# Spreading the side work of the attention stage over its pairs, on a kernel of three transformer layers and a rotation

## The chip, the cores and the metric

The kernel runs on one core of a Trainium2 chip. The metric is the device time of one execution in microseconds, as a median of several runs. Before the change it is 1247.71 us (three runs, 1241.72 to 1253.38).

Five engines work side by side and wait for each other by semaphores: TensorE (PE for its matmuls, PEld for its weight loads), VectorE (DVE), ScalarE (ACT), GpSimd (POOL) and SyncE (SP), which only issues transfers here. On each engine the instructions run in the order in which they are written.

## The reference

The input is x, 32 batches of 128 rows with 144 columns, and a condition vector per batch. Three layers follow each other, each of an attention part and an MLP part, then a rotation:

```python
ada = silu(c) @ W_ada + b_ada                    # shift, scale, gate for both parts
h = modulate(layernorm(x), shift_msa, scale_msa)
x = x + gate_msa * attention(h, ...)             # 16 heads of width 9
h = modulate(layernorm(x), shift_mlp, scale_mlp)
x = x + gate_mlp * mlp(h)                        # 144 -> 576 -> 144, gelu
# layer 1 has four experts of that size with a top-2 router instead of one MLP
x_rot = x + ((x @ U) @ expm(A(c)) - x @ U) @ U.T # U from a QR of P
```

## The kernel before, in words

Layers are numbered l = 0, 1, 2. The order of work on every engine is written out by hand; no scheduler moves anything. x stays in SBUF for the whole program. POOL computes U during most of the program and takes no part in the attention.

**Attention** of a layer works through 16 pairs of batches, i = 0 to 15, e = 2i and o = 2i + 1 being the two batches. Each of the three busy engines has a function `pair` (DVE from L577, ACT from L1150, PE later in the file). It is a software pipeline: in pair i the scores of batches 2i and 2i+1 are computed, while the output of the batches two to four before is transposed, normalised, projected and added to x, and the inputs of the batches up to four ahead are prepared. In one pair

- PE does the scores of e and o twice (L1472 for the row maxima, L1479 for the softmax), the products with the values (L1496), transposes (L1457, L1507, L1517, L1522), the product that makes q, k and v of the next pair (L1415) and the projection (L1527, L1528);
- DVE takes the row maxima in four `row_max` reductions of 1024 columns (L547), two for e and two for o. After the second of a batch PE transposes the maxima (L1507) and DVE adds them to the queries (`max_row`, L555); the second kind of scores of that batch waits for this. In between stand the low halves of operands (L514, L515, L542), the normalisation of coming batches (`normalise`, L508 and L511), the output's normalisation (L564, L569) and gating (L519), and the update of x with its statistics (L524, L527);
- ACT takes four exponentials of 1024 columns (L1135), and copies and rounds everything that PE has made. `qk_double` (L1118) is the copy that PE needs before it transposes the second batch's queries and keys (`qk_turned`, L1457).

Three pieces of work that belong to other parts are put between the pairs:

- **MLP weights.** They are split into a high and a low part for the products. `mlp_cast` (L1045) on ACT rounds a quarter of the weights, two instructions per call (L1051 for 128 rows, L1052 for the last 51), called after pairs 2 to 5. `mlp_split` (L457) on DVE makes the low part of a quarter, two instructions per call (L463, L464), called after pairs 3 to 6. In layers 0 and 2 a quarter is 144 columns wide, in layer 1, with its four experts, 577.
- **Deviations.** `deviation` (L467) makes mean and reciprocal deviation of 16 batches from their statistics, in 13 steps k = 0 to 12 of one to three small instructions, each step waiting for the one before. In pair 1 it runs for the second half of the batches of this attention, in pair 11 for the first half of the batches of the coming MLP; its steps stand one by one between the other operations of the pair (`step(k)`).
- **The MLP's second group of rows.** `rows(1, 1, ...)` normalises batches 4 to 7 for the MLP (two of them after pair 14, two after pair 15; one batch is one L508 and one L511).

After the last pair comes `passage`, in which the pipeline runs empty and the MLP's first products start. PE there waits for the transposed rows of the second group and for all weight splits (`m_split`). SP waits for the weight splits too, before it loads the next layer's weights, but behind a loop that follows the last updates of x.

Of the kernel before, what the change touches and what calls it, by code (L numbers as in the profile page):

```python
# [16 lines left out]
S3 = 3 * C1  # L17
# [42 lines left out]
def program(nc, d, out, gates_dram, skew_dram):  # L60
    ctx = ExitStack()
    with ctx:
# [319 lines left out]
        def _(dve):  # L382
# [73 lines left out]

            def mlp_split(l, q):  # L457

                n = WM[l]
                wr, wr3 = raw(n)  # L460
                at = slice(q * n // 4, (q + 1) * n // 4)
                dve.wait_ge(m_cast, 2 * (4 * l + q + 1))
                V.tensor_tensor(Mlo[:, at], wr[:, at], Mhi[:, at].bitcast(F32), ALU.subtract).then_inc(m_split, 1)  # L463
                V.scalar_tensor_tensor(MW3[0:S3, at], MW3[0:S3, at].bitcast(F32), K[0:S3, K_MW:K_MW + 1], wr3[:, at],  # L464
                                       ALU.mult, ALU.add).then_inc(m_split, 1)

# [62 lines left out]
            def attention(l):  # L529
# [46 lines left out]

                def pair(i, dev=None, stats=None, late=None):  # L577

# [18 lines left out]
                    if at(2):  # L597
                        gated_at(e - 4, e % 4)
                    step(2)
                    if at(0):  # L600
                        row_max(e, 1)
# [7 lines left out]
                    if at(-1):  # L609
                        qk_low(NP * l + i + 1, 0)  # L610
                    step(5)
                    if at(0):
# [30 lines left out]
                    if at(-1):  # L643
                        qk_low(NP * l + i + 1, 1)
                    if dev:
                        dve.wait_ge(s_ln, 10 * rstd_part(*dev) + 10)
# [334 lines left out]
            for l in range(LAYERS):  # L981
# [22 lines left out]
                for i in range(NP):  # L1004
                    pair(i, late=late if l == 2 and i == 0 else None, dev=(l, 0, 1) if i == 1 else (l, 1, 0) if i == 11 else None)
                    if l == 0 and i == 0:
                        columns_rest()
                    if i in (3, 4, 5, 6):
                        mlp_split(l, i - 3)
                    if i >= NP - 2:  # L1010
                        rows(1, 1, range(2 * (i - NP + 2), 2 * (i - NP + 3)))
                passage(rows, low, ones)
# [6 lines left out]
        def _(act):  # L1019
# [24 lines left out]

            def mlp_cast(l, q):  # L1045
                n = WM[l]
                wr, wr3 = raw(n)
                at = slice(q * n // 4, (q + 1) * n // 4)
                act.wait_ge(ld_wm, 112 * (l + 1))
                act.wait_ge(s_const, 3)  # L1050
                S.activation(Mhi[:, at], wr[:, at], ACT.Copy).then_inc(m_cast, 1)  # L1051
                S.activation(MW3[0:S3, at], wr3[:, at], ACT.Copy).then_inc(m_cast, 1)  # L1052

# [20 lines left out]
            def attention(l):  # L1074
# [74 lines left out]

                def pair(i, rest=None):  # L1150

# [19 lines left out]
                    if at(0):  # L1171
                        qk_copy(pn, 3)
                    if at(-1):
                        qkv_high(pn + 1, 0)
                        qk_double(pn + 1, 0)
# [167 lines left out]
            for l in range(LAYERS):  # L1343
                pair = attentions[l][0]
                gelus, modulate, cast, step = mlp(l, attentions[l + 1] if l + 1 < LAYERS else None)
                if l == 0:
                    pair(-2)
                    pair(-1)
                for i in range(NP):
                    pair(i, rest=setup_rest if l == 0 and i == 0 else None)  # L1350
                    if i in (2, 3, 4, 5):
                        mlp_cast(l, i - 2)
                attentions[l][6](gelus, modulate, cast)
                for m in range(NM + 2 * (l == LAYERS - 1)):
                    step(m, m % 2)
# [722 lines left out]
```

## Time and profile before

| what | us |
|---|---|
| median of 3 runs | 1247.71 (1241.72 to 1253.38) |
| the profiled execution, its own time | 1246.81 |
| its span in the trace | 1244.7 |
| busy: PE, PEld, DVE, ACT, POOL | 1174.2, 940.0, 906.7, 784.9, 739.9 |
| first row maximum of pairs 0 and 15, layer 0 | 34.1 and 223.6 |
| the same in layer 1 | 340.3 and 527.9 |
| the same in layer 2 | 904.1 and 1090.3 |

The profile is one execution. The distance between the first row maxima (L547) of two following pairs is the length of a pair. A window of the trace lists for a stretch of time the busy time of each engine, the TensorE clock that was granted as a share of 2.4 GHz (1.00 or 0.50, 0.50 being 1.2 GHz), and the use of the DMA engines. In a timeline row stand start, duration, engine, line and operation, and in square brackets the idle time before it and what ended that. Ends of PE rows are modelled, so its busy time is not all work. Instructions of one engine overlap by some 0.08 us where neither waits for the other.

### The profile page before, as it was taken

To read this page: it belongs to the slowest core of one execution; us is meant where nothing else is said; L and a number is where in the kernel's file an instruction comes from. 1 tells how busy PE (TensorE), PEld (TensorE's weight loads), DVE (VectorE), ACT (ScalarE), POOL (GpSimd) and SP (SyncE) were. 2 spreads that over 40 slices of the span, in tenths; PEclk is the share of its full clock that TensorE was granted. 3 is DMA by queue.
4 is the path that set the end of the run, shared out by engine and by line. 5 is a ranking of instruction groups with operands and counts; after the bars stand their busy time and mean duration, and the time that the engine had idled before them with its cause. 6 is when DMAs were issued, how large, how long until landed. Compare 5 with 4: busy or idle time off the path is not lost.

```text
span 1244.7 us, 35644 instructions
## 1 busy us (share of the span) xinstructions
PE 1174.2 (94%) x12868; PEld 940.0 (76%) x12868; DVE 906.7 (73%) x2505; ACT 784.9 (63%) x1809; POOL 739.9 (59%) x2230
## 2 busy tenths in 40 slices
PE   6899999989989999999999999999989999998997
PEld 3677777678766777768888888888867777767885
DVE  6899999866489999965565565556489999965432
ACT  3589898856489898962332442342479898955551
POOL 5665665665565666666666666667777777770000
PEclk8899999999999999999999999999999999979997
DMA  6322112243441121221111111120031111100121
GB/s 175 63 16 21 19 19 21 46 101 36 87 89 20 17 20 18 20 59 6 14 14 6 15 15 6 14 47 11 20 61 32 25 33 33 33 8 16 24 60 37
DMA packets 50353, 42.85 MB, mean 34 GB/s; under 512 B 8487, under 2 KB 45786, under 8 KB 49749
## 3 DMA queue, kind: packets, MB, share of 16 engines
q1 hardware_dynamic: 45916, 29.91, 10.8%
q0 software_dynamic: 3488, 8.52, 8.6%
q8 instruction: 105, 1.72, 0.5%
q10 hardware_dynamic: 780, 2.17, 0.5%
q14 instruction: 64, 0.52, 0.1%
HBM read 33.86 MB, written 3.03 MB: 30 GB/s over the span
## 4 chain that ended last, share of the span: by engine, by line
PE 80%; DVE 14%; issue 4%; ACT 1%; DMA 0%; SPq 0%; DVEq 0%; ACTq 0%
PE PS L1700 18%; PE PSA L1415 14%; PE PS L1496 7%; PE PSA L1472 7%; PE PS L1457 7%; PE PS L1415 6%; DVE BIG L547 3%; PE PSB L1673 2%; PE PS L1527 2%; PE PS L1517 2%; PE PS L1528 2%; PE PSB L1479 1%; PE PS L1522 1%; PE PS L1507 1%; DVE xh L511 1%
## 5 line engine op out<-in xcount | busy, mean ns | idle before, releaser
L1266 ACT ACTIVATE BIG<-PSA 128x512 f32<-128x512 f32 (+1 forms) x224 | 132.5, 594 | 265.3 <-PE PSA L1415 265.1
L1700 PE MATMUL PS<-w,BIG 128*128 128x144 f32 (+1 forms) x1920 | 254.7, 287 | 7.2 <-DVE BIG L821 3.6
L1700 PEld LDWEIGHTS PS<-w,BIG 128*128 128x128 f32 (+1 forms) x1920 | 245.2, 190 | 14.7 <-DVE BIG L821 4.5
L547 DVE TENSOR_REDUCE BIG<-PSA 128x8 f32<-128x1024 f32 x192 | 234.2, 1220 | 28.2 <-PE PSA L1472 26.1
L1135 ACT ACTIVATE BIG<-PSB 128x1024 f32<-128x1024 f32 x192 | 195.5, 1018 | 19.5 <-PE PSB L1479 19.3
L1472 PEld LDWEIGHTS PSA<-KK,Q 32*128 32x128 f32 x1536 | 104.8, 188 | 56.7 <-issue 41.2
L1472 PE MATMUL PSA<-KK,Q 32*128 32x128 f32 x1536 | 129.3, 284 | 16.1 <-DVE BIG L547 3.7
L1479 PE MATMUL PSB<-Q,KK 32*128 32x128 f32 x1536 | 129.7, 287 | 0.0
L1923 POOL MEMSET qprod<- 128x2 f32 x63 | 6.6, 104 | 205.2 <-DMA VB<-QA 205.2
L1457 PE MATMUL PS<-K,qt 128*128 128x128 f32 x768 | 120.9, 282 | 7.9 <-DVE qt L542 3.3
L1496 PE MATMUL PS<-BIG,VA 128*32 128x128 f32 x3072 | 125.4, 282 | 1.7 <-DVE col L422 1.7
L1905 POOL TENSOR_TENSOR qtree<-qtree 128x36 f32<-128x36 f32 (+3 forms) x384 | 100.6, 262 | 30.1
L1457 PEld LDWEIGHTS PS<-K,qt 128*128 128x128 f32 x768 | 87.2, 142 | 31.4 <-DVE qt L542 15.9
L821 DVE SCALAR_TENSOR_TENSOR BIG<-PS,BIG 128x144 f32<-128x144 f32 x96 | 34.9, 367 | 94.6 <-PE PS L1700 94.0
L1479 PEld LDWEIGHTS PSB<-Q,KK 32*128 32x128 f32 x1536 | 102.5, 189 | 1.4 <-issue 0.7
L1415 PE MATMUL PSA<-hhi,Mhi 128*128 128x512 f32 (+1 forms) x224 | 100.2, 447 | 2.9 <-DVE h L515 2.0
L1910 POOL TENSOR_TENSOR qtree<-qtree 128x4 f32<-128x4 f32 (+3 forms) x384 | 80.4, 209 | 30.0
L1496 PEld LDWEIGHTS PS<-BIG,VA 128*32 128x32 f32 x3072 | 73.1, 110 | 29.0 <-issue 19.2
L1415 PE MATMUL PSA<-h,MW 128*128 128x512 f32 (+1 forms) x224 | 88.8, 397 | 0.0
L1415 PE MATMUL PSA<-hhi,Mlo 128*128 128x512 f32 (+1 forms) x224 | 88.8, 396 | 0.0
L1415 PE MATMUL PSA<-hlo,Mhi 128*128 128x512 f32 (+1 forms) x224 | 88.3, 394 | 0.0
L1110 ACT ACTIVATE qt<-PS 128x288 fp32r<-128x288 f32 x93 | 41.3, 444 | 50.5 <-PE PS L1415 50.5
(309 smaller groups left out, 2941.7 us busy)
## 6 DMA issues: line engine op xcount, KB each, us to landing
gate<-gates SPq DMA_DIRECT2D x96, 72.0 KB, 2.9
mgate<-gates SPq DMA_DIRECT2D x96, 72.0 KB, 2.7
VB<-skew POOLq DMA_DIRECT2D x16, 288.0 KB, 3.7
X<-in_x SPq DMA_DIRECT2D x4, 576.0 KB, 9.7
out<-X SPq DMA_DIRECT2D x8, 288.0 KB, 3.6
BIG<-in_skew_w SPq DMA_DIRECT2D x2, 1024.0 KB
w<-in_w SPq DMA_DIRECT2D x1, 1440.0 KB, 10.1
BIG<-in_wqkv SPq DMA_DIRECT2D x2, 584.0 KB
```

The lines of the kernel that those rows point to most:

```text
L547: V.tensor_reduce(nmax.rearrange("p (s w) -> p s w", w=HP)[:, 2 * a:2 * a + 2, 3 * HD:3 * HD + G], PSA[:, :].rearrange("p (r g k) -> p r g ...
L1110: S.activation(qt[:, s, :, :, 0:HD], src, ACT.Copy).then_inc(qk_hi, 1)
L1135: S.activation(PT[:, u % 2, a, :], PSB[:, :], ACT.Exp, scale=float(HD) ** -0.5).then_inc(exp_done, 1)
L1266: S.activation(hm[0:rows, slot, :], PS[(par * FTOT[l] + j) % 2][0:rows, :], gelu).then_inc(gelu_done, 1)
L1415: last = mm(o, a, b, start=(k == 0), stop=(k == 3))
L1457: last = nc.tensor.transpose(turn_bank(pn, j)[:, g * 128:(g + 1) * 128], qt[:, s, j % 2, 4 * g:4 * g + 4, :].rearrange("p h w -> p (h w)") ...
L1472: one = mm(PS[r][:, g * 128:(g + 1) * 128], Q[rows, par, g, q0:q0 + 128], KK[rows, par, g, q0:q0 + 128], start=True, stop=True)
L1479: two = mm(PS[2 + r][:, g * 128:(g + 1) * 128], KK[rows, par, g, q0:q0 + 128], Q[rows, par, g, q0:q0 + 128], start=True, stop=True)
L1496: last = mm(PS[6][p0:p0 + HP, at:at + 128], VA[:, u, G * g + 2 * a + r, :], PT[:, u % 2, a, (G * r + g) * 128:(G * r + g + 1) * 128], star ...
L1700: last = mm(o, hm[0:rows, slot, s * 128:(s + 1) * 128], w2[0:rows, FT * e + k, :], start=(k == 0), stop=(k == FT - 1))
L1905: link(R.tensor_tensor(t[:, 0:n, :], a[:, :, 0:half], a[:, :, half:2 * half], ALU.add))
L1910: link(R.tensor_tensor(t[:, 0:n, :], a[:, :, 0:half], a[:, :, half:2 * half], ALU.add))
```

## The change

Each piece of side work is put inside `pair`, in smaller portions:

- `mlp_cast` and `mlp_split` take an index n8 of 0 to 7 and issue one instruction per call. The casts run in pairs 2 to 9, ahead of the copy of the next pair's queries (`qkv_high(pn + 1, 0)`); the splits run in pairs 3 to 10, ahead of the second row maximum of e.
- `deviation` for the coming MLP runs in pairs 10 to 13, with steps 0-3, 4-6, 7-9 and 10-12, all steps of a pair in one place: behind the split, ahead of the second row maximum of e. In layers 1 and 2 the deviation of the attention's second half runs so in pairs 1 to 4. In layer 0 that one stays in pair 1, step by step.
- All four batches of `rows(1, 1, ...)` are normalised in pair 15: two of them ahead of `max_row(e)`, two at the end of the pair.

```diff
-            def mlp_split(l, q):
-
-                n = WM[l]
+            def mlp_split(l, n8):
+
+                q, n = n8 // 2, WM[l]
                 wr, wr3 = raw(n)
                 at = slice(q * n // 4, (q + 1) * n // 4)
-                dve.wait_ge(m_cast, 2 * (4 * l + q + 1))
-                V.tensor_tensor(Mlo[:, at], wr[:, at], Mhi[:, at].bitcast(F32), ALU.subtract).then_inc(m_split, 1)
-                V.scalar_tensor_tensor(MW3[0:S3, at], MW3[0:S3, at].bitcast(F32), K[0:S3, K_MW:K_MW + 1], wr3[:, at],
-                                       ALU.mult, ALU.add).then_inc(m_split, 1)
+                dve.wait_ge(m_cast, 8 * l + n8 + 1)
+                if n8 % 2 == 0:
+                    V.tensor_tensor(Mlo[:, at], wr[:, at], Mhi[:, at].bitcast(F32), ALU.subtract).then_inc(m_split, 1)
+                else:
+                    V.scalar_tensor_tensor(MW3[0:S3, at], MW3[0:S3, at].bitcast(F32), K[0:S3, K_MW:K_MW + 1], wr3[:, at],
+                                           ALU.mult, ALU.add).then_inc(m_split, 1)
...
                     if at(2):
                         gated_at(e - 4, e % 4)
                     step(2)
+                    if split is not None:
+                        mlp_split(l, split)
+                    if devs:
+                        for k in range(*devs[3]):
+                            deviation(*devs[:3], k)
+                        if devs[3][1] == 13:
+                            dve.wait_ge(s_ln, 10 * rstd_part(*devs[:3]) + 10)
                     if at(0):
                         row_max(e, 1)
...
                     if at(-1):
                         qk_low(NP * l + i + 1, 0)
+                    if rows:
+                        rows(1, 1, range(2))
                     step(5)
                     if at(0):
                         max_row(e, e % 4)
...
                         qk_low(NP * l + i + 1, 1)
+                    if rows:
+                        rows(1, 1, range(2, MT))
...
                 for i in range(NP):
-                    pair(i, late=late if l == 2 and i == 0 else None, dev=(l, 0, 1) if i == 1 else (l, 1, 0) if i == 11 else None)
+                    k0 = i - 1 if l and 1 <= i < 5 else i - 10
+                    devs = (l, int(i >= 10), int(i < 10), (0, 4, 7, 10, 13)[k0:k0 + 2]) if 0 <= k0 < 4 else None
+                    pair(i, late=late if l == 2 and i == 0 else None, dev=(l, 0, 1) if i == 1 and l == 0 else None,
+                         devs=devs, split=i - 3 if 3 <= i < 11 else None, rows=rows if i == NP - 1 else None)
                     if l == 0 and i == 0:
                         columns_rest()
-                    if i in (3, 4, 5, 6):
-                        mlp_split(l, i - 3)
-                    if i >= NP - 2:
-                        rows(1, 1, range(2 * (i - NP + 2), 2 * (i - NP + 3)))
...
                     if at(0):
                         qk_copy(pn, 3)
+                    if cast is not None:
+                        mlp_cast(l, cast)
                     if at(-1):
                         qkv_high(pn + 1, 0)
                         qk_double(pn + 1, 0)
...
-                    pair(i, rest=setup_rest if l == 0 and i == 0 else None)
-                    if i in (2, 3, 4, 5):
-                        mlp_cast(l, i - 2)
+                    pair(i, rest=setup_rest if l == 0 and i == 0 else None, cast=i - 2 if 2 <= i < 10 else None)
```

What this does to the order of instructions is seen at three places. The first is ACT in layer 1, at the end of a pair with a cast before the change (Mhi and MW are the high parts of the weights, KK and qt the keys and queries); here the two casts stand ahead of L1118, `qk_double`:

```order
L1110 ACTIVATE qt<-PS 128x32x9
L1111 ACTIVATE VA<-PS 128x2x8x9
L1051 ACTIVATE Mhi<-BIG 128x577
L1052 ACTIVATE MW<-BIG 51x577
L1097 ACTIVATE hhi<-hf 128x256
L1098 ACTIVATE hshi<-hs 51x256
L1118 ACTIVATE qt<-qt 128x2x16x9
```

With the change, one cast stands between the copy of the keys and that of the next queries (line numbers have shifted by 13 or 14: L1064 is the cast, L1124 and L1125 are `qkv_high`, L1132 is `qk_double` of the first batch):

```order
L1155 ACTIVATE BIG<-PS 128x256
L1139 ACTIVATE KK<-PS 128x4x128
L1064 ACTIVATE Mhi<-BIG 128x577
L1124 ACTIVATE qt<-PS 128x32x9
L1125 ACTIVATE VA<-PS 128x2x8x9
L1132 ACTIVATE qt<-qt 128x2x16x9
L1149 ACTIVATE BIG<-PSB 128x1024
```

The cast has moved from the end of the pair to its first half, and each pair has one instead of two. The second place is DVE in pair 10 of layer 1 after the change, where a split (L466) and four steps of the deviation (L475 to L490) stand ahead of the second row maximum (L549). Before the change L519, the gating, was followed there by L547 at once:

```order
L521 TENSOR_TENSOR ytmp<-PS,gate 128x144
L466 SCALAR_TENSOR_TENSOR MW<-MW,K,BIG 51x577
L475 TENSOR_TENSOR mean<-st 128x16
L476 TENSOR_TENSOR rtmp<-st 128x16
L477 TENSOR_TENSOR var<-st 128x16
L480 TENSOR_SCALAR mean<-mean 128x16
L481 TENSOR_SCALAR var<-var 128x16
L482 TENSOR_TENSOR rtmp<-rtmp 128x16
L485 SCALAR_TENSOR_TENSOR var<-rtmp,var 128x16
L489 TENSOR_SCALAR rtmp<-var 128x16
L490 TENSOR_SCALAR var<-var 128x16
L549 TENSOR_REDUCE BIG<-PSA 128x2x4
```

So ten instructions have come between the gating and the row maximum. The third place is DVE in pair 15 of layer 0. Before, with two batches normalised ahead of the pair's first row maximum (they are not shown), the second row maximum of e was followed by:

```order
L547 TENSOR_REDUCE BIG<-PSA 128x2x4
L564 RECIPROCAL BIG<-PS 128x16
L569 TENSOR_TENSOR BIG<-PS,BIG 128x144
L555 TENSOR_TENSOR Q<-Q,PS 128x4x128
L508 TENSOR_SCALAR xh<-X,mean,rstd 128x128
L511 TENSOR_SCALAR xh<-X,mean,rstd 128x3x16
```

With the change it is:

```order
L549 TENSOR_REDUCE BIG<-PSA 128x2x4
L566 RECIPROCAL BIG<-PS 128x16
L571 TENSOR_TENSOR BIG<-PS,BIG 128x144
L510 TENSOR_SCALAR xh<-X,mean,rstd 128x128
L513 TENSOR_SCALAR xh<-X,mean,rstd 128x3x16
L510 TENSOR_SCALAR xh<-X,mean,rstd 128x128
L513 TENSOR_SCALAR xh<-X,mean,rstd 128x3x16
L557 TENSOR_TENSOR Q<-Q,PS 128x4x128
```

The four instructions of the MLP's first two batches have moved behind the second row maximum and ahead of L557, `max_row` of batch 30.

## Rows read from the trace of the kernel before

**Rows 1.** Page: span, and TensorE's granted clock in 40 slices of the span.

```profile
span 1244.7 us, 35644 instructions
...
PEclk8899999999999999999999999999999999979997
```

**Rows 2.** Windows: stretch, length, busy PE, PEld, DVE, ACT, POOL, then PEclk, DMA, GB/s.

```profile
441.55:477.92 36.37, 35.85 (x526) 27.63 (x529) 33.52 (x79) 32.42 (x80) 22.87 (x69) 1.00 0.16 18
...
63.73:210.57 146.84, 143.75 (x2092) 110.46 (x2088) 139.00 (x338) 130.81 (x320) 88.86 (x253) 1.00 0.22 19
352.38:514.88 162.50, 154.43 (x2254) 118.30 (x2257) 152.49 (x374) 144.17 (x344) 100.57 (x299) 1.00 0.17 18
917.48:1076.72 159.24, 154.51 (x2254) 118.30 (x2256) 150.78 (x375) 141.44 (x344) 124.56 (x411) 1.00 0.14 32
```

**Rows 3.** Timeline, an undisturbed pair of layer 1 (DVE, PEld, ACT).

```profile
455.55 0.29 DVE L519 TENSOR_TENSOR ytmp<-PS,gate 128x144 f32<-128x144 f32 x1
456.37 1.23 DVE L547 TENSOR_REDUCE BIG<-PSA 128x8 f32<-128x1024 f32 x1 [0.53 <-PE PSA L1472]
...
458.66 0.20 PEld L1457 LDWEIGHTS PS<-K,qt 128*128 128x128 f32 x2 [0.27 <-DVE qt L542]
...
457.35 0.45 ACT L1110 ACTIVATE qt<-PS 128x288 fp32r<-128x288 f32 x1 [0.99 <-PE PS L1415]
```

**Rows 4.** Timeline, layer 1, casts and what PE waits for (ACT, PE).

```profile
388.70 0.70 ACT L1051 ACTIVATE Mhi<-BIG 128x577 fp32r<-128x577 f32 x1
...
390.46 0.46 ACT L1118 ACTIVATE qt<-qt 128x288 fp32r<-128x288 f32 x1
...
391.02 0.30 PE L1457 MATMUL PS<-K,qt 128*128 128x128 f32 x1 [0.76 <-issue]
```

**Rows 5.** Timeline of DVE, splits of a quarter in layer 1.

```profile
389.72 0.75 DVE L463 TENSOR_TENSOR Mlo<-BIG,Mhi 128x577 fp32r<-128x577 f32 x1
390.38 0.80 DVE L464 SCALAR_TENSOR_TENSOR MW<-MW,K,BIG 51x577 fp32r<-51x577 f32 x1
```

**Rows 6.** Groups by line, DVE in 60 to 235 us: the splits of layer 0.

```profile
L464 DVE SCALAR_TENSOR_TENSOR MW<-MW,K,BIG 51x144 fp32r<-51x144 f32 x4 | 1.8, 445 | 0.0
L463 DVE TENSOR_TENSOR Mlo<-BIG,Mhi 128x144 fp32r<-128x144 f32 x4 | 1.2, 310 | 0.0
```

**Rows 7.** Timeline of DVE: a deviation alone, starts of steps 0, 4 and 7.

```profile
262.89 0.16 DVE L473 TENSOR_TENSOR mean<-st 128x16 f32<-128x16 f32 x1
...
264.16 0.19 DVE L493 TENSOR_TENSOR rtmp<-rtmp 128x16 f32<-128x16 f32 x1
...
264.82 0.17 DVE L493 TENSOR_TENSOR rtmp<-rtmp 128x16 f32<-128x16 f32 x1
```

**Rows 8.** Timeline, pair 15 of layer 0 up to the passage (DVE, PE).

```profile
222.64 0.34 DVE L508 TENSOR_SCALAR xh<-X,mean,rstd 128x128 f32<-128x128 f32 x1
...
223.58 1.21 DVE L547 TENSOR_REDUCE BIG<-PSA 128x8 f32<-128x1024 f32 x1
...
227.28 0.69 DVE L555 TENSOR_TENSOR Q<-Q,PS 128x512 fp32r<-128x512 f32 x1
...
249.93 0.31 DVE L527 BATCH_NORM_STATS2 st<-X 128x6 f32<-128x144 f32 x1
...
228.23 0.29 PE L1472 MATMUL PSA<-KK,Q 32*128 32x128 f32 x1 [0.36 <-DVE Q L555]
```

**Rows 9.** Timeline of DVE, the same two places in layer 2.

```profile
1093.96 0.68 DVE L555 TENSOR_TENSOR Q<-Q,PS 128x512 fp32r<-128x512 f32 x1
...
1122.93 0.31 DVE L527 BATCH_NORM_STATS2 st<-X 128x6 f32<-128x144 f32 x1
```

**Rows 10.** Windows in pair 15, of layer 2 (two) and of layer 0.

```profile
1090.60:1094.00 3.40, 2.24 (x38) 1.26 (x36) 3.37 (x8) 1.86 (x3) 2.67 (x10) 1.00 0.08 14
1094.00:1111.10 17.10, 16.89 (x131) 12.71 (x131) 11.68 (x32) 8.99 (x18) 13.50 (x45) 0.50 0.07 10
227.00:230.40 3.40, 2.66 (x35) 1.90 (x35) 3.35 (x10) 1.80 (x4) 0.19 (x1) 1.00 0.46 19
```

More of the change, by code:

```diff
@@ L575, in update, with pair @@
                     added(n_gated(l, 0) + b, n_batch(l, 0) + b, b)
-                def pair(i, dev=None, stats=None, late=None):
+                def pair(i, dev=None, stats=None, late=None, devs=None, split=None, rows=None):
                     def at(lag):
@@ L1043, in _, with mlp_cast @@
                 load_rows(act, AC1[l], d["ada_col"][:, l * AC:(l + 1) * AC], ld_ada)
-            def mlp_cast(l, q):
-                n = WM[l]
+            def mlp_cast(l, n8):
+                q, n = n8 // 2, WM[l]
                 wr, wr3 = raw(n)
@@ L1050, in mlp_cast @@
                 act.wait_ge(s_const, 3)
-                S.activation(Mhi[:, at], wr[:, at], ACT.Copy).then_inc(m_cast, 1)
-                S.activation(MW3[0:S3, at], wr3[:, at], ACT.Copy).then_inc(m_cast, 1)
+                if n8 % 2 == 0:
+                    S.activation(Mhi[:, at], wr[:, at], ACT.Copy).then_inc(m_cast, 1)
+                else:
+                    S.activation(MW3[0:S3, at], wr3[:, at], ACT.Copy).then_inc(m_cast, 1)
             def qkv_cast(l):
@@ L1148, in oT_copy, with pair @@
                     S.activation(oT[0:C1, u % 2, 128:256], tail_bank(b)[0:C1, 128:256], ACT.Copy).then_inc(oT_ev, 1)
-                def pair(i, rest=None):
+                def pair(i, rest=None, cast=None):
                     def at(lag):
```

## The prediction

> **What bounds the kernel now.** I read the windows over the attention stages first, then the timelines of single pairs, and the granted clock last. Three pairs without side work take 36.37 us, 12.12 each; PE is busy for 35.85 of them, and DVE and ACT for 33.5 and 32.4 [rows 2]. So PE sets the pair, and the other two have some slack, which counts only at the places where it lies. On DVE 0.53 us lie ahead of the second row maximum of e, waiting for PE; since instructions overlap by about 0.08, work of up to 0.60 us fits there free of charge [rows 3]. Behind that reduction there is none: PE waits 0.27 us for the low halves that DVE makes two steps later, so what comes ahead of the reduction beyond 0.60 delays PE one for one [rows 3]. On ACT 0.99 us lie ahead of `qkv_high`, waiting for PE's product [rows 3].
>
> The side work shows as time above 12.12 us a pair. Layer 0 takes 146.84 us for its 12 pairs 2 to 13, 1.40 too many; layers 1 and 2 take 162.50 and 159.24 for the 13 pairs 1 to 13, 4.94 and 1.68 too many [rows 2]. These 8.0 us are all that casts, splits and deviations can give back in these stretches. Pairs 14 and 15 are a matter of their own, and there stands the clock: it falls to half in the 36th slice [rows 1], from 1094.00 to 1111.1 us, in pair 15 and the passage of layer 2 and in no other attention stage [rows 10].
>
> **Casts.** Two casts in layer 1 stand from 388.70 on, ahead of `qk_double`, which starts at 390.46; PE's transpose of its result had to wait 0.76 us [rows 4]. That is most of layer 1's loss, four times. One cast of 0.70 us in the new place lies in the idle 0.99 us ahead of `qkv_high` [rows 3, 4]: no cost. In layers 0 and 2 the casts are a quarter as wide and fit as well. If that cover were gone, each would cost its 0.70 us eight times over.
>
> **Splits.** A split of layer 1 takes 0.66 us (389.72 to 390.38) or, for the second kind, 0.80 less the overlap, 0.72 [rows 5]. Alone in the 0.60 it costs 0.06 or 0.12. Those of layers 0 and 2, 0.23 and 0.36 after the same deduction [rows 6], fit. The splits now finish in pair 10 instead of after pair 6; PE and SP ask for them only in the passage, behind the updates of the last batches, so nothing waits for that.
>
> **Deviations.** Where a deviation runs alone, step 4 starts 1.27 us after step 0, and the next three steps take 0.66 [rows 7]. In front of a reduction that does not depend on them the last wait falls away, so I take 1.15 for steps 0-3 and 0.52 for each other portion. 0.52 alone fits into the 0.60.
>
> Per layer, in excess over 12.12 us:
>
> - Layer 0: pair 10 has a split of 0.36 and 1.15, less 0.60: 0.91. Pairs 3 to 9 and 11 to 13: nothing. Sum 0.9 against 1.40: a gain of 0.5.
> - Layer 1: pairs 3 and 4 have a split and three steps, 0.66 + 0.52 - 0.60 = 0.58 and 0.64; pairs 5 to 9 0.06, 0.12, 0.06, 0.12, 0.06; pair 10 0.72 + 1.15 - 0.60 = 1.27. Sum 2.9. Pair 1 carries steps 0-3 in a pair whose pipeline is not full, which no row shows: between nothing and 1.15, and I take 0.3, since the same steps lay in this pair before. 3.2 against 4.94: a gain of 1.7.
> - Layer 2: pair 1 0.3; pairs 3 and 4 0.23 + 0.52 - 0.60 = 0.15 and 0.28; pair 10 0.91. Sum 1.6 against 1.68: nothing.
>
> Together a gain of 2.3 us.
>
> **The second group's rows.** Before, the two batches after pair 14 took DVE from 222.64 to 223.58, 0.94 us, and delayed the first row maximum of pair 15 [rows 8]. But DVE then ran without a break up to `max_row` of batch 30 at 227.28, for which PE waited 0.36 us until 228.23 [rows 8]. Now DVE comes to the pair 0.94 earlier, meets the idle time ahead of the second reduction (0.53 [rows 3], hidden before by the lateness), and does the same 0.94 us between that reduction and `max_row(30)`. So `max_row(30)` and the scores of batch 31 come later: by at least 0.53, by at most 0.94; I take 0.7, the middle, and this in layers 0 and 1. It stays, for DVE is the late one up to the end of the pair. In layer 2 the two batches took 0.6 longer before (they are part of what put `max_row` at 1093.96 [rows 9]), so the same shift should leave about 0.1 there. Loss 1.5 us. The two batches after pair 15 stay where they were.
>
> **Without the clock** the sum is -2.3 + 1.5 = -0.8 us: 1246.0 against the profiled execution's 1246.81. That execution lies 0.9 below the median of the runs shown.
>
> **The clock.** In layer 2 it fell after a stretch of 3.40 us in which PE was busy for 2.24; in layer 0 at the same place it was 2.66 of 3.40, and it did not fall [rows 10]. What the fall costs follows from equal work in both layers: from `max_row(30)` to the last statistics of the passage 227.28 to 249.93, 22.65 us in layer 0, and 1093.96 to 1122.93, 28.97 us in layer 2 [rows 8, 9]: 6.3 us. The change moves PE's idle time of pair 15 together: the same few matmuls now stand before a wait of 0.36 + 0.94 = up to 1.3 us at one place, in all three layers. Take 0.7 us off the 2.66 of layer 0 and 1.96 are left; PE would then have done less there than it did in layer 2 before the fall. The runs of before, 1241.72, 1247.71 and 1253.38, lie 6 us apart, as if none, one and two stages had been hit. My forecast is that one stage more than in the profiled execution is hit: 1246.0 + 6.3 = 1252.3 us.
>
> The section "HAM oscillation — how this bites in real kernels" of the page TensorE: Matmul & The Clock Gate in the Trainium skill ties such falls to waits on transfers that leave TensorE wholly idle for long; waits of 1.3 us between matmuls would be harmless by it, and the sum would stay 1246.0. The row from layer 2 speaks against it, where the clock fell although PE was busy for two thirds.
>
> **Rivals.**
>
> 1. *The pair keeps its clock as before* (one stage hit or its like): 1246.0. For it: layers 0 and 1 ran through waits in pair 15 without a fall; whether it falls may hang on chance, since it differed between layers with the same work. Against it: PE will be idle for longer than where it fell. The Trainium skill's rule above gives the same time. 0.36.
> 2. *All stages fall*, ending clearly slower: the wait of PE for `max_row(30)` makes all three passages run at 1.2 GHz, two more than before, 1246.0 + 12.6 = 1258.6. It decides from the point where the wait grows by 0.5 us or more in every layer, so that PE does less there than in the stretch of layer 2 before the fall. For it: the work is the same in each layer. Against it: the shift may be only 0.53 us. 0.16.
> 3. *No stage falls*: the first reduction of pair 15 is no longer late, PE keeps busy up to there, and that is enough even in layer 2: 1246.0 - 6.3 = 1239.7. 0.08.
> 4. *The deviations hurt more*: if each wait between steps also delays PE because `gated_at` ends later than in the rows, every 0.52 costs in full: ten portions, about 5 us on top of 1246.0, 1251. Against it: the idle 0.53 us is there in each undisturbed pair. 0.04.
>
> My forecast has the remaining 0.36, and comes first because the idle time in pair 15 is the one thing that surely grows.
>
> **Numbers.** 1252.3 us. Range 1240 to 1259: it takes in rivals 1 to 4, with a rest below and above for the scatter of the clock. A change of 1%, 12.5 us of 1247.7, is about what a measurement of this kernel can tell from none. Faster by more than that would be under 1235.2, below even rival 3: 0.02. Slower would be over 1260.2, which takes rival 2 with another 1.6 us: 0.06. Within 1%: 0.92.
>
> **What would show it.** In layer 1, pairs 5 to 9 at 12.2 us, and no wait of PE ahead of the transpose behind `qk_double`; pair 10 about 1 us long in every layer beyond 12.12; pairs 11 to 13 at 12.12; in pair 15 a wait of PE for `max_row(30)` of about 1 us or more, and behind it a granted clock of 0.50 in two of the three stages. The prediction is wrong if that wait is no longer than 0.4 us, if the clock stays at 1.00 in all passages although it grew, or if the stretches of pairs 1 to 13 give back much more or less than 2.3 us.

## The result, and the profile after

The changed kernel takes 1257.11 us (median of 14 runs, 1246.63 to 1261.28), the kernel before 1246.24 (14 runs, 1236.18 to 1253.38): ratio 1.0083, 95% interval 1.0058 to 1.0108, so 10.9 us are lost. The forecast was 1252.3 in a range of 1240 to 1259. Of the runs told below, two of the kernel with the moved rows alone and one of the kernel before in two sessions count as slow (over 1.5% above the fastest of their kernel); medians and ranges include them, ratios leave them out.

The page of the changed kernel's profiled execution (1260.5 us by its own time), to be read beside [rows 1]:

```profile
span 1258.2 us, 35656 instructions
...
PE 77%; DVE 15%; issue 5%; ACT 1%; DMA 0%; SPq 0%; DVEq 0%; ACTq 0%
...
PEclk9899999789999999979999999999999999979999
```

Of the ends of the three attention stages only slice 36 showed a 7 before; now slices 8, 18 and 36 do. All stretches at half clock within the span come to 73 us, against 48 in the profiled execution of before.

Windows over the same stages as in [rows 2], then, for pair 15 of each layer, the 3.4 us before the fall and the stretch behind it (columns as in [rows 2]; the third from the end is the granted clock), as in [rows 10]:

```profile
61.30:207.90 146.60, 143.65 (x2092) 110.39 (x2088) 140.45 (x339) 131.75 (x321) 88.33 (x253) 1.00 0.22 19
361.20:522.10 160.90, 155.11 (x2256) 118.32 (x2253) 155.12 (x375) 146.02 (x343) 99.61 (x300) 1.00 0.18 18
932.90:1092.50 159.60, 154.87 (x2254) 118.12 (x2250) 152.39 (x374) 142.62 (x343) 124.78 (x413) 1.00 0.14 32
222.20:225.60 3.40, 2.17 (x37) 1.19 (x33) 2.86 (x8) 1.95 (x4) 2.92 (x9) 1.00 0.03 4
225.60:242.70 17.10, 16.42 (x129) 12.50 (x129) 10.83 (x33) 8.78 (x16) 9.16 (x25) 0.50 0.46 70
536.20:539.60 3.40, 2.38 (x38) 1.40 (x37) 2.84 (x8) 2.10 (x5) 1.01 (x4) 1.00 0.35 24
539.60:556.70 17.10, 15.69 (x127) 12.29 (x128) 10.31 (x28) 8.55 (x16) 11.59 (x37) 0.50 0.31 65
1109.70:1113.10 3.40, 1.85 (x28) 1.55 (x28) 3.40 (x9) 1.74 (x5) 2.75 (x9) 1.00 0.00 0
1113.10:1126.80 13.70, 13.70 (x117) 10.12 (x121) 8.64 (x28) 7.85 (x17) 5.44 (x17) 0.50 0.06 12
```

The pairs give back a little: 1.16 us over 12.12 a pair in layer 0, 3.34 in layer 1, 2.04 in layer 2, together 6.5 where it was 8.0. The fall in pair 15 takes it away several times over. In layer 0 of before the granted clock had stayed at 1.00 at this place.

The timeline of DVE in pair 15 of layer 0 of the changed kernel, then of PE (start, duration, instruction, and in brackets the wait), to be read beside [rows 8]:

```profile
220.02 1.22 DVE L549 TENSOR_REDUCE BIG<-PSA 128x8 f32<-128x1024 f32 x1
...
222.71 1.23 DVE L549 TENSOR_REDUCE BIG<-PSA 128x8 f32<-128x1024 f32 x1 [0.53 <-PE PSA L1486]
...
224.36 0.34 DVE L510 TENSOR_SCALAR xh<-X,mean,rstd 128x128 f32<-128x128 f32 x1
...
225.08 0.36 DVE L513 TENSOR_SCALAR xh<-X,mean,rstd 128x48 f32<-128x48 f32 x1
225.36 0.66 DVE L557 TENSOR_TENSOR Q<-Q,PS 128x512 fp32r<-128x512 f32 x1
```

```profile
224.66 0.27 PE L1537 MATMUL PS<-K,BIG 128*17 128x128 f32 x1
226.28 0.44 PE L1486 MATMUL PSA<-KK,Q 32*128 32x128 f32 x1 [1.35 <-DVE Q L557]
```

DVE now meets its idle 0.53 us, does the four instructions, and PE waits 1.35 us for `max_row` (L557) of batch 30, where it was 0.36. The waits in layers 1 and 2 are 1.87 (539.14 to 541.01) and 1.32 (1109.54 to 1110.86), so the clock fell within the wait in layers 0 and 1, and 2.2 us after it in layer 2. In the middle of the wait of layer 0, at 225.60, the clock goes down, and the scores behind it, at 0.44 us instead of 0.29, are the first to be slow.

The span is 13.5 us longer. From the first row maximum of layer 0 to that of layer 1 it is 315.2 us (33.85 to 349.09) instead of 306.2; from there to layer 2 (918.80) 569.7 instead of 563.8; from there to the end 339.4 instead of 340.5, since both executions have a fall there. So the time sits in the two stages that fell newly: 9.0 us in the stretch of layer 0, which has a second fall of 6.8 us at 273.4, and 5.9 in that of layer 1.

### The profile page after: what moved, and what is told of

Same layout as the page of the kernel before. It is cut to its first block, busy times and chain, and to the rows that moved or that the text cites. A ratio compares the mean times of both kernels' runs of the same rounds, so it can differ in the third digit from the quotient of the medians.

```text
span 1258.2 us, 35656 instructions
## 1 busy us (share of the span) xinstructions
PE 1187.6 (94%) x12868; PEld 951.3 (76%) x12868; DVE 914.3 (73%) x2505; ACT 789.4 (63%) x1809; POOL 741.7 (59%) x2230
## 4 chain that ended last, share of the span: by engine, by line
PE 77%; DVE 15%; issue 5%; ACT 1%; DMA 0%; SPq 0%; DVEq 0%; ACTq 0%
PE PS L1714 18%; PE PSA L1429 14%; PE PSA L1486 7%; PE PS L1510 7%; PE PS L1471 6%; PE PS L1429 5%; DVE BIG L549 3%; PE PSB L1687 2%; PE PS L1541 2%; PE PS L1531 2%; PE PS L1542 1%; PE PSB L1493 1%; PE PS L1536 1%; DVE xh L513 1%; PE PS L1521 1%
## 5 line engine op out<-in xcount | busy, mean ns | idle before, releaser
L1714 PE MATMUL PS<-w,BIG 128*128 128x144 f32 (+1 forms) x1920 | 257.6, 289 | 7.3 <-DVE BIG L834 3.5
L1714 PEld LDWEIGHTS PS<-w,BIG 128*128 128x128 f32 (+1 forms) x1920 | 247.9, 192 | 15.6 <-DVE BIG L834 4.6
L549 DVE TENSOR_REDUCE BIG<-PSA 128x8 f32<-128x1024 f32 x192 | 234.2, 1220 | 21.4 <-PE PSA L1486 19.7
L1493 PE MATMUL PSB<-Q,KK 32*128 32x128 f32 x1536 | 133.1, 292 | 0.0
L1510 PE MATMUL PS<-BIG,VA 128*32 128x128 f32 x3072 | 128.6, 287 | 1.7 <-DVE col L422 1.7
L1919 POOL TENSOR_TENSOR qtree<-qtree 128x36 f32<-128x36 f32 (+3 forms) x384 | 103.5, 269 | 30.1
L1493 PEld LDWEIGHTS PSB<-Q,KK 32*128 32x128 f32 x1536 | 105.4, 193 | 2.0 <-issue 2.0
L557 DVE TENSOR_TENSOR Q<-Q,PS 128x512 fp32r<-128x512 f32 x96 | 65.4, 681 | 5.9 <-PE PS L1521 1.6
## 6 DMA issues: line engine op xcount, KB each, us to landing
X<-in_x SPq DMA_DIRECT2D x4, 576.0 KB, 10.2
```

Of the source, the lines that this page charges most:

```text
L549: V.tensor_reduce(nmax.rearrange("p (s w) -> p s w", w=HP)[:, 2 * a:2 * a + 2, 3 * HD:3 * HD + G], PSA[:, :].rearrange("p (r g k) -> p r g ...
L557: V.tensor_tensor(q, q.bitcast(F32), PS[5][:, 0:128].rearrange("p (o n) -> p o n", o=1).broadcast_to([128, G, 128]), ALU.add).then_inc(mro ...
L1493: two = mm(PS[2 + r][:, g * 128:(g + 1) * 128], KK[rows, par, g, q0:q0 + 128], Q[rows, par, g, q0:q0 + 128], start=True, stop=True)
L1510: last = mm(PS[6][p0:p0 + HP, at:at + 128], VA[:, u, G * g + 2 * a + r, :], PT[:, u % 2, a, (G * r + g) * 128:(G * r + g + 1) * 128], star ...
L1714: last = mm(o, hm[0:rows, slot, s * 128:(s + 1) * 128], w2[0:rows, FT * e + k, :], start=(k == 0), stop=(k == FT - 1))
L1919: link(R.tensor_tensor(t[:, 0:n, :], a[:, :, 0:half], a[:, :, half:2 * half], ALU.add))
```

## The experiments

Each was timed in 12 runs beside the kernel before, whose medians in those sessions were 1246.0 to 1247.9 us. Of each kernel one execution was profiled; "us at half clock" below is (1 - mean granted clock) x span x 2, as a mean over all its runs. It is 69 for the change (14 runs) and 43 for the kernel before (35 runs; 41 to 50 over the four sessions).

### The moved rows alone, and all but them

Before, with only the rows moved into pair 15:

```diff
                     if at(-1):
                         qk_low(NP * l + i + 1, 0)
+                    if rows:
+                        rows(1, 1, range(2))
                     step(5)
...
                         qk_low(NP * l + i + 1, 1)
+                    if rows:
+                        rows(1, 1, range(2, MT))
...
-                    if i >= NP - 2:
-                        rows(1, 1, range(2 * (i - NP + 2), 2 * (i - NP + 3)))
```

> The kernel before with one part of the change done: only the rows move into pair 15. Theory A: PE waits about 1.3 us for max_row(30) in each layer, the clock falls there in all three layers, and the time is 11 to 13 us above the kernel before, about 1258 us. Rival B: the rows alone cost 1.5 us, about 1248 us.

Measured 1254.65 us (1242.51 to 1265.79), ratio 1.0071 (1.0032 to 1.0109), less than theory A's 11 to 13 us above before. The other half, the change with the same edit undone:

> The changed kernel with one part undone: the MLP's second group of rows is normalised after pairs 14 and 15 again; casts, splits and deviations stay as changed. Theory A (the rows put TensorE's idle time of pair 15 together, and the clock falls to half there in all three layers): PE's wait for max_row(30) goes back from 1.35 to about 0.4 us, the clock keeps 1.00 in the passages of layers 0 and 1, and the time is that of the kernel before less the 2.3 us of the other parts, about 1244 us. Rival B (the portions of deviations and splits cost more than they give back and the falls come by chance): it stays at 1254 to 1257 us.

Measured 1246.78 (1242.69 to 1259.54), ratio 1.0016 (0.9978 to 1.0054). The moved rows carry the loss: alone they give 7 to 9 of the 11 us (by the medians and by the ratio), and without them it is gone. The 1244 of theory A was not reached. Us at half clock: 62 and 49.

In the profile of the rows alone, windows in pair 15 of layer 0 and of layer 1, the 3.4 us up to the end of PE's wait or to the fall, then what follows:

```profile
220.40:223.80 3.40, 1.54 (x25) 0.73 (x23) 3.37 (x10) 1.33 (x3) 2.70 (x9) 1.00 0.00 0
223.80:240.90 17.10, 15.33 (x186) 11.52 (x187) 13.38 (x40) 12.83 (x28) 11.30 (x33) 1.00 0.38 69
...
529.30:532.70 3.40, 1.39 (x27) 0.68 (x19) 3.37 (x10) 0.96 (x3) 1.68 (x6) 1.00 0.02 1
532.70:539.50 6.80, 6.80 (x76) 5.01 (x73) 5.20 (x12) 4.38 (x9) 5.37 (x18) 0.50 0.08 13
```

PE waited in layer 0 as it did after the change:

```profile
223.77 0.29 PE L1475 MATMUL PSA<-KK,Q 32*128 32x128 f32 x1 [1.30 <-DVE Q L555]
```

and the clock stayed, although PE had been busy for only 1.54 of the 3.4 us. So a wait of this length does not bring the fall each time, and how busy PE was just before does not decide it alone. The falls of this execution in pair 15 were short, 6.8 us in layer 1 and 3.4 in layer 2, and its span, 1240.3 us, lies far below the median of its kernel.

### Fillers on TensorE in pair 15

Is it the clock or the wait itself? The change, with n matmuls on an unused result ahead of the scores of batch 31, so that PE works where it waited (`keep_warm` is a function that the kernel had, and `PS[0]` a bank that nobody reads then):

```diff
                     if i == 0:
                         keep_warm(PS[2], 2)
+                    if i == NP - 1:
+                        keep_warm(PS[0], 3)        # 5 in the first kernel, 3 in the second
                     if at(-1):
                         qk_turned(i + 1, 0)
```

> The changed kernel, in which PE issues five matmuls of 256 columns into a free bank while it waits for max_row(30) in pair 15 (added work whose result nobody reads); nothing else moves. It takes the idle time away and leaves the wait. Theory A: the clock stays at 1.00 in pair 15 and the passage of all three layers, the time falls to that of the kernel before less 0.8 us or lower, 1240 to 1245 us. A rival C, that the wait itself and not the clock costs the time, and rival B expect no gain: 1256 to 1259 us.

> The changed kernel with three matmuls of 256 columns instead of five in PE's wait for max_row(30) of pair 15. Five took 2.32 us in a wait of 1.35 and so delayed the scores by about 0.9 us in each layer; three take 1.4 us. The clock should still stay at 1.00 there, and the time should be 2 to 3 us below the one with five matmuls, about 1243 us. If the clock falls again, about 1250 us.

Measured with five: 1245.46 (1240.46 to 1251.99), ratio 0.9986 (0.9956 to 1.0017). With three: 1243.87 (1240.21 to 1251.22), ratio 0.9978 (0.9947 to 1.0009). The first is 0.5 us above the range of theory A, the second 0.9 above its forecast; both are far from the 1256 to 1259 of the rivals. Windows of the kernel with three, layer 0, the 3.4 us up to `max_row(30)` and 17.1 behind it, and the fillers on PE:

```profile
221.77:225.17 3.40, 2.84 (x42) 2.01 (x41) 3.07 (x9) 2.10 (x5) 2.99 (x8) 1.00 0.06 9
225.17:242.27 17.10, 15.35 (x185) 11.21 (x184) 14.30 (x42) 12.00 (x27) 10.16 (x27) 1.00 0.46 72
```

```profile
224.62 1.46 PE L1409 MATMUL PSA<-K 128*128 128x256 f32 x6
```

`max_row` starts at 225.17, 5.06 us after the pair's first row maximum, against 5.34 in the changed kernel. From the first row maximum of pair 14 (207.75) it is 17.42 us, against 17.46 in the changed kernel and 16.71 in the kernel before. So `max_row` is as late as there, but the clock does not fall, and 13.2 us come back. Us at half clock: 34 and 33.

The same three fillers with the moved rows alone, with all but the rows, and with nothing of the change (that with casts and splits alone, told below, stands in the table too):

> The kernel before with only the rows of the second group moved into pair 15, and the same three filler matmuls there. Theory A (what the moved rows cost, 7 us alone, is the clock at 1.2 GHz behind pair 15): 1247 us, within 3 of before. Theory B (it is the later max_row of batch 30 itself that costs): 1254, as without the fillers.

> The change with its rows as they were before, and the three filler matmuls in pair 15. Theory A (clock alone): the rows' place no longer matters once the fillers are there, so the time is that of the change with fillers, 1244 within 2 us. Theory B (the rows' place costs beside the clock): 2 us or more below it, 1241.

> The kernel before with nothing but the three filler matmuls in pair 15 of each layer. Theory A (beside the clock the change moves nothing that can be measured): 1244 us within 1.5, the same as the whole change with the fillers, so its gain in the pairs of layer 1 shows as at most 1 us. Theory B (the whole change gives back 2 us once the clock is out of the way): 1246. Theory C (the fillers cost the kernel before something, since it rarely fell there): 1248.

| kernel | without fillers, us | with three | ratio to before, with three |
|---|---|---|---|
| before | 1246.0 to 1247.9 | 1244.68 | 0.9968 (0.9945 to 0.9991) |
| rows alone | 1254.65 | 1243.67 | 0.9980 (0.9949 to 1.0012) |
| all but the rows | 1246.78 | 1244.23 | 0.9992 (0.9962 to 1.0022) |
| casts and splits alone | 1247.52 | 1243.81 | 0.9977 (0.9951 to 1.0003) |
| the whole change | 1257.11 | 1243.87 | 0.9978 (0.9947 to 1.0009) |

With fillers all five lie within about 1 us, as theory A had it in these three (for the rows alone even 3 us better). What makes the change slower is the clock in pair 15 and behind it; whatever else the change does is smaller than the intervals of some 3 us to either side.

One more wait has to be read beside this table. Early in the MLP of layer 2, PE transposes U for the rotation (`u_turn`, L1744 in the kernel before), and POOL must have finished U for that. POOL's last instruction for it is a MEMSET that tells PE so. Here it is in the changed kernel, without and with three fillers, and behind each PE's transpose; then that transpose in the kernel before and in the kernel with casts and splits alone:

```profile
1119.74 0.10 POOL L1983 MEMSET qexponents<- 128x1 f32 x1
1148.07 0.27 PE L1758 MATMUL PSB<-K,UT 64*128 64x64 f32 x1
...
1134.80 0.10 POOL L1985 MEMSET qexponents<- 128x1 f32 x1
1134.96 0.36 PE L1760 MATMUL PSB<-K,UT 64*128 64x64 f32 x1 [9.53 <-POOL qexponents L1985]
...
1132.79 0.27 PE L1744 MATMUL PSB<-K,UT 64*128 64x64 f32 x1
...
1130.19 0.27 PE L1749 MATMUL PSB<-K,UT 64*128 64x64 f32 x1 [2.64 <-POOL qexponents L1974]
```

POOL was done between 1119.8 and 1134.9 us in the 14 profiles. In five of them PE came first and waited, 2.6 to 9.5 us: all but the rows (6.4), casts and splits without and with fillers (2.6 and 4.8), the spread rows with fillers told below (5.1), and the whole change with three fillers (9.5). From that transpose to the end of the span it is 108 to 112 us in every profile. So what is gained earlier counts only until POOL is done: in the execution with 9.5 us of waiting, work ahead of it that was up to 9.5 us shorter would not have made the span of 1243.2 us any shorter. In the changed kernel without fillers PE comes 28 us after POOL, so its loss counts in full. No experiment moved POOL's work, so how much of a gain this wait hides in the medians stays open; the small differences of the table are not a measure of what the parts of the change are worth.

The rows alone with fillers, in the windows around pair 15 and the passage of the three layers:

```profile
220.00:245.00 25.00, 22.30 (x276) 16.44 (x274) 20.39 (x60) 18.29 (x42) 15.23 (x45) 1.00 0.34 54
520.00:560.00 40.00, 37.18 (x413) 27.94 (x412) 29.70 (x88) 30.40 (x69) 24.73 (x76) 1.00 0.25 49
1085.00:1115.00 30.00, 27.45 (x347) 20.42 (x346) 25.72 (x69) 23.52 (x54) 23.70 (x77) 1.00 0.09 22
```

and the changed kernel at those places:

```profile
220.00:245.00 25.00, 23.09 (x220) 17.39 (x220) 16.90 (x47) 13.97 (x29) 15.29 (x44) 0.66 0.35 53
520.00:560.00 40.00, 37.36 (x447) 28.15 (x445) 28.94 (x71) 27.48 (x62) 25.28 (x76) 0.79 0.25 39
1085.00:1125.00 40.00, 37.38 (x473) 28.35 (x473) 33.79 (x83) 30.66 (x68) 27.64 (x90) 0.85 0.09 20
```

Counted over all profiles, pair 15 and its passage saw a fall in 11 of 21 stages of the seven kernels without fillers there (both originals and five variants), and in none of 21 of the seven with them. Of the 11, five fell in the 6 stages of the two kernels with the rows moved as in the change, and six in the 15 of the others.

### The rows spread out

The change, with one batch ahead of the second row maximum of pair 14, one in pair 15 there, where 0.53 us are idle, and two at the end:

```diff
+                    if rows:                       # rows is given in pairs 14 and 15
+                        rows(1, 1, range(i - NP + 2, i - NP + 3))
                     if at(0):
                         row_max(e, 1)
...
-                    if rows:
-                        rows(1, 1, range(2))
...
```

(The last portion is done in pair 15 only, and PE's wait for the turned rows counts the new order.)

> The changed kernel with the four batches of rows spread: one ahead of the second row maximum of e in pair 14, one there in pair 15, two at the end of pair 15. Each 0.5 us portion stands in the idle 0.6 us. Theory A: max_row(30) comes at its natural time, PE waits for it 0.3 us or less, no clock falls in pair 15 in any layer, and the time is below both kernels: 2.3 us from the other parts, about 0.9 us a layer from pair 14, and the fall that the kernel before has in some stages: 1236 to 1243 us. Rival B: 1253 to 1256 us.

Measured 1247.03 (1241.53 to 1253.99), ratio 1.0003 (0.9968 to 1.0039), 49 us at half clock: 10 below the change, but not below before. PE's wait for `max_row(30)` is back at 0.37 us, and still the clock fell in layer 0:

```profile
227.12 0.38 PE L1486 MATMUL PSA<-KK,Q 32*128 32x128 f32 x1 [0.37 <-DVE Q L557]
```

```profile
223.80:227.20 3.40, 2.47 (x42) 1.51 (x42) 3.32 (x9) 2.10 (x5) 2.73 (x9) 1.00 0.02 4
227.20:234.00 6.80, 6.80 (x75) 5.16 (x75) 4.86 (x11) 4.08 (x10) 3.08 (x9) 0.50 0.28 23
```

My expectation had taken the short wait for a safe one, and that was wrong. With this arrangement, one filler in pair 15 and two in pair 0 of layers 1 and 2:

> The kernel with the rows spread (one in pair 14, one in pair 15, two behind), and in it added matmuls of 256 columns where PE waits: one in pair 15 ahead of the scores of batch 31 (a wait of 0.37 us), two in pair 0 of layers 1 and 2 ahead of the second scores of batch 1 (a wait of 1.27 us). Theory A (time follows how long the clock is at half, about 0.4 us for each us of it): the falls at the start of layers 1 and 2 and in pair 15 become rarer, the mean time at half clock goes from 49 us to 35 or less, the time to about 1241 us. If the falls have another cause, it stays at 1247.

Measured 1244.39 (1238.99 to 1250.91), ratio 0.9982 (0.9952 to 1.0012), 36 us at half clock: no better than three fillers in the changed kernel. The 13 us less at half clock came with 2.6 us less time, 0.2 for each, where theory A had taken 0.4; its 1241 was not reached.

### The rest of the change

Casts and splits as in the change, all else as before, without and with the three fillers:

> The kernel before with one part of the change done: casts and splits one instruction per pair; deviations and rows as before. By the sums of the prediction: layer 1's pairs 1 to 13 give back about 3.4 us of their 4.94, layer 0 and 2 about 0.5 each; a gain of 4.4 us, 1242.8 against 1247.2, if the clock falls as often as before. If the cast was not what held layer 1 up, the gain is under 1 us.

> The kernel before with the change's casts and splits, and three filler matmuls of 256 columns on TensorE in pair 15 of each layer, ahead of the scores of batch 31. Theory A (spreading casts and splits shortens the pairs by about 5 us, but the 1.2 GHz stretches took that away again when they stood alone): with the falls in pair 15 gone the shorter pairs show, 1242 us, 5 below before. Theory B (the pairs get shorter but the end of the stage gives it back whatever the clock): 1247, as casts and splits alone.

Measured 1247.52 (1240.92 to 1255.06), ratio 1.0014 (0.9978 to 1.0050), and 1243.81 (1241.46 to 1245.48), ratio 0.9977 (0.9951 to 1.0003). The pairs of layer 1 did become shorter in both, here in the one without and the one with fillers (pairs 1 to 13, before 162.50 in [rows 2]):

```profile
353.60:513.50 159.90, 154.75 (x2254) 118.23 (x2256) 153.94 (x375) 146.00 (x344) 99.22 (x297) 1.00 0.17 18
```

```profile
352.60:512.00 159.40, 154.97 (x2257) 118.27 (x2258) 152.91 (x375) 145.58 (x344) 98.65 (x292) 1.00 0.18 19
```

That is 2.6 and 3.1 us in layer 1 alone, and neither time shows it; neither 1242.8 nor theory A's 1242 with fillers was reached. Two things stand against the gain. The first kernel was at half clock for 59 us, the second for 36, against 43 and 30 of their counterparts; in the first the clock fell in pair 15 of two layers behind waits of only 0.36 us. That shorter pairs themselves make falls more likely fits these numbers, but no run shows it. And in both profiles PE then waited for POOL's U, 2.6 and 4.8 us. Which of the two takes how much is open.

Deviations alone:

> The kernel before with one part of the change done: deviations in four pairs, all steps of a pair in one place; the rest as before. By the sums of the prediction steps 0-3 cost 0.55 us in pair 10 (no split stands there), the other portions fit into idle time: 0.6 us a layer against 0.9, 0.6 and 1.0 before, about 1 us faster or the same. If every portion delays TensorE in full, 5 us slower.

Measured 1245.35 (1239.18 to 1251.01), ratio 0.9979 (0.9952 to 1.0006), 34 us at half clock: no difference that can be told. Its pair 15 is that of before. In layer 0 the clock fell all the same, at 225.1, even before PE's wait of 0.21 us for `max_row(30)` began; ahead of it stood only waits of 0.48, 0.37 and 0.18 us. So this place is exposed without any of the moved rows:

```profile
225.77 0.44 PE L1479 MATMUL PSA<-KK,Q 32*128 32x128 f32 x1 [0.21 <-DVE Q L555]
```

```profile
221.70:225.10 3.40, 2.32 (x38) 1.38 (x37) 3.37 (x8) 1.81 (x3) 2.80 (x10) 1.00 0.03 6
225.10:242.20 17.10, 16.89 (x131) 12.50 (x130) 11.00 (x33) 9.23 (x18) 10.93 (x30) 0.50 0.34 66
```

## Why the prediction was right or wrong

**Casts: right.** PE's idle time ahead of the transposes behind `qk_double` was 4.2 us in pairs 1 to 13 of layer 1 (3.0 of it without a named releaser), and is 0.1 now. Groups by line of before and of after, PE, over these pairs (busy, mean ns, then idle time and what ended it):

```profile
L1457 PE MATMUL PS<-K,qt 128*128 128x128 f32 x208 | 32.4, 279 | 4.2 <-issue 3.0 <-DVE qt L542 1.1
```

```profile
L1471 PE MATMUL PS<-K,qt 128*128 128x128 f32 x208 | 32.6, 280 | 0.1
L1521 PE MATMUL PS<-K,BIG 128*128 128x128 f32 x26 | 7.8, 299 | 1.8 <-DVE BIG L549 1.7
```

With a cast ahead of `qkv_high`, ACT still had 0.42 us of idle time there (at 414.66). The second row of after is the transpose of the row maxima, where PE did not wait before (0.0) and now waits for the later second row maximum: that is the price of splits and deviations.

**Splits and deviations: right in kind, a little too cheap.** DVE in pair 10 of layer 1 after the change, from the first row maximum of the pair to that of the next:

```profile
472.39 1.22 DVE L549 TENSOR_REDUCE BIG<-PSA 128x8 f32<-128x1024 f32 x1
...
474.48 0.80 DVE L466 SCALAR_TENSOR_TENSOR MW<-MW,K,BIG 51x577 fp32r<-51x577 f32 x1
475.21 0.17 DVE L475 TENSOR_TENSOR mean<-st 128x16 f32<-128x16 f32 x1
...
476.34 1.22 DVE L549 TENSOR_REDUCE BIG<-PSA 128x8 f32<-128x1024 f32 x1
...
485.73 1.21 DVE L549 TENSOR_REDUCE BIG<-PSA 128x8 f32<-128x1024 f32 x1
```

The split takes 0.73 and the four steps 1.13 us, where I had 0.72 and 1.15; the pair is 13.34 long, 1.22 over, where I had 1.27. Pairs 5 to 9 take 12.28 each (410.99 to 472.39) instead of 12.2, pairs 11 to 13 12.11 each (485.73 to 522.07). The sum in excess of 12.12 is 6.5 us in place of 5.7, so the gain is 1.5, not 2.3. What is missing lies where the small portions were put at nothing: pair 2 takes 12.41 us in layer 1 and 12.43 in layer 2, pair 11 of layer 2 12.39.

**The rows: right in layer 0, short in layer 1.** From the first row maximum of pair 14 to `max_row(30)` it is 17.46 us in layer 0, 17.99 in layer 1 and 17.44 in layer 2, against 16.71, 16.71 and 17.24: 0.75, 1.28 and 0.20 more, where I had 0.7, 0.7 and 0.1. In layer 1 the second batch's L513 took 0.60 us instead of 0.36, and its wait became the longest. Together 2.2, not 1.5. With the pairs that is +0.7 us in these two executions where the forecast had -0.8; the medians with fillers, 1243.87 after and 1244.68 before, say -0.8, and their intervals of about 3 us to either side hold both.

**The clock: the right mechanism, mis-sized.** The term that came out too small is the last: "one stage more than in the profiled execution is hit: 1246.0 + 6.3". In the profiled execution of the change two stages more were hit, all three, which is rival 2's case with its 1258.6 against 1260.5. Over the runs the change spends 69 - 43 = 26 us more at half clock. By my own price, 6.3 us for a fall of 17.1 us [rows 8 to 10], that is 1.5 falls and 9.6 us of the 10.9 lost. A fit of time on us at half clock over the 14 runs of the change gives 0.39 us for each (standard error 0.04), and 10.2 for 26; the fillers took 36 us and 13.2 us of time away, 0.37 for each. But that is not the price everywhere: over the 116 runs of the kernel before beside the experiments the same fit gives 0.25, by which 26 us would be 6.6. A part of what a fall costs there may hide behind the wait for POOL, which is open. The price holds in the new profile: layer 1 has a single fall and became 5.9 us longer. What I had wrong was to treat the number of stages as a whole number read from one execution, when it is a chance per stage. In the profiles without fillers 5 of 6 stages fell with the rows moved (rows alone and the change) and 6 of 15 without. So few stages would not show alone that the longer wait raises the chance; the 62 and 69 us at half clock over the runs, against 34 to 59 of the five others, and the fillers do. The reading that the clock fell "in no other attention stage" of before was not quite right either: it also fell for 3.4 us at 49.5, in pair 0 of layer 0.

**The rivals.** Rival 1 said 1246.0, on the ground that waits of 1.3 us do no harm. By the rule of the Trainium skill that I set beside it (page TensorE: Matmul & The Clock Gate, section "HAM oscillation — how this bites in real kernels"), gaps of this length are safe. The traces disagree: the clock fell within waits of 1.35 and 1.87 us and 2.2 us after one of 1.32, in two variants just behind waits of 0.36 and 0.37, and in a third among waits of 0.48 us and less, with PE busy for 2.3 to 2.5 of the 3.4 us before. Rival 3, that no stage falls, is what the fillers bring about, at 1243.87 rather than 1239.7, because falls in pairs 0 and 1, in the MLP and in the rotation remain and because PE can then be earlier than POOL; the forecast had no term for that wait. Rival 4 is excluded by the deviations alone, 1245.35.

## What to carry to other kernels

Where the matmul engine has been full for a hundred microseconds, a wait can cost far more than its length: scores that came 0.2 to 1.3 us later in each layer cost 11 us here, most of it through the clock. Before putting work on the engine that it waits for, look at the granted clock behind that place in several executions, since one can show none, one or three falls. If the wait must stay, a few matmuls on unused data in front of it are worth trying: three per layer took all the loss back, and the kernel before with them came out 0.3% faster (ratio 0.9968, 0.9945 to 0.9991), a small gain; the five kernels with them, 1243.67 to 1244.68 us, cannot be told apart. When several kernels end at the same time, look for a wait that they share before calling their differences nothing: here PE can be stopped in all of them by POOL's U.

## What the runs showed of the hardware

- The granted clock went to half for 3.4, 6.8, 10.2, 13.7 or 17.1 us at a time, and the same kernel had different falls in different executions: in the profile of the rows alone a wait of 1.30 us ended without a fall in layer 0, and one of 1.45 in layer 1 was followed by a fall of 6.8 us.
- 1 us at half clock costs the changed kernel 0.37 to 0.39 us (6.3 for 17.1 in the profile of before; the fit over 14 runs of the change), and 0.25 in the fit over 116 runs of the kernel before. That is less than the 0.5 of work that PE does not do in it; I take it that PE has some slack, which no run shows.
- POOL, which does the same work in all 14 profiles, was done with U between 1119.8 and 1134.9 us. In each of the five profiles in which PE waited for it, for 2.6 to 9.5 us, the granted clock fell during the wait or 1.2 us after it.
- The three fillers show as six records of 256 columns and 1.46 us on PE, and delayed nothing by an amount that the median shows.
